# A gated block on one Trainium2 core: VectorE's calls in the block-product stage put in a new order, and two tiles of a down product added by one operation

## What is computed

```python
def _L0_ffn_ref(x, W_up, W_gate, W_down):
    wu, wg, wd = ternary_quant(W_up), ternary_quant(W_gate), ternary_quant(W_down)   # 2048x512, 2048x512, 512x2048
    up = jnp.einsum('bsd,ed->bse', x, wu)
    gate = jnp.einsum('bsd,ed->bse', x, wg)
    hidden = jax.nn.silu(up) * gate
    return jnp.einsum('bse,de->bsd', hidden, wd)
x = x + jnp.tanh(g_xattn[0]) * _L0_xattn_ref(_layernorm(x), ctx_1024, Wq, bq, Wk, bk)   # x: 4 x 512 x 512
x = x + jnp.tanh(g_ffn[0]) * _L0_ffn_ref(_layernorm(x), W_up, W_gate, W_down)
```

## Time and profile before

| | us |
|---|---|
| median of 3 runs (lowest, highest) | 394.8 (394.6, 394.83) |
| span of the profiled execution | 393.2 |
| TensorE busy | 388.2 |
| VectorE busy | 330.2 |
| ScalarE busy | 269.8 |
| GpSimd busy | 183.9 |
| granted TensorE clock, mean | 1.000 |

### The profile page before, as it was taken

The page is one execution under the profiler, slowest core; times in us unless marked ns, Lnnn a source line. Parts: engine busy times, 40 slices in busy tenths (PEclk is TensorE's granted clock), DMA queues, the critical chain, the costliest instruction groups (busy, mean ns, idle before and its releaser), DMA issues.

```text
span 393.2 us, 6214 instructions
## 1 busy us (share of the span) xinstructions
PE 388.2 (99%) x2000; PEld 219.3 (56%) x2000; DVE 330.2 (84%) x501; ACT 269.8 (69%) x366; POOL 183.9 (47%) x199
## 2 busy tenths in 40 slices
PE   8999999999999999999999999999999999999997
PEld 6676775554444444444444444556545665656886
DVE  0778897988799975789888979999999989798974
ACT  3887988899777786869897982856287566564400
POOL 0498727767845031403169462643639447261000
DMA  8999977799600030020029470006230000000014
GB/s 287 404 402 407 408 232 184 176 261 183 160 2 0 1 108 0 13 96 0 2 60 190 86 148 2 0 1 214 78 139 0 2 1 2 0 2 1 2 61 154
DMA packets 44048, 43.91 MB, mean 112 GB/s; under 512 B 30833, under 2 KB 33009, under 8 KB 42993
## 3 DMA queue, kind: packets, MB, share of 16 engines
q1 hardware_dynamic: 44016, 43.53, 36.3%
HBM read 29.89 MB, written 6.29 MB: 92 GB/s over the span
## 4 chain that ended last, share of the span: by engine, by line
PE 84%; DVE 6%; ACT 4%; issue 4%; DMA 1%; POOL 1%; DVEq 0%; ACTq 0%; POOLq 0%
PE pair L924 20%; PE pair L926 20%; PE pair L1052 14%; PE pair L1000 8%; PE pair L815 7%; PE pair L838 6%; PE pair L788 4%; PE pair L772 3%; PE pair L799 2%; DVE x_sb L1855 1%; DVE xf L1804 1%; DMA xf<-in_first 1%; PE pair L853 1%; DVE sh L1814 1%; ACT xf L1395 1%
## 5 line engine op out<-in xcount | busy, mean ns | idle before, releaser
L924 PE MATMUL pair<-xb_hi,w_sb 128*128 128x512 f16 x448 | 169.8, 379 | 0.9 <-DVE xf L1799 0.5
L926 PE MATMUL pair<-xb_lo,w_sb 128*128 128x512 f16 x448 | 169.8, 379 | 0.0
L924 PEld LDWEIGHTS pair<-xb_hi,w_sb 128*128 128x128 fp8e4 x448 | 43.8, 98 | 54.0 <-DVE xf L1799 1.3
L926 PEld LDWEIGHTS pair<-xb_lo,w_sb 128*128 128x128 fp8e4 x448 | 43.8, 98 | 49.5 <-issue 0.3
L1344 ACT ACTIVATE xf<-xf,small 128x512 f32<-128x512 f32 x48 | 34.5, 720 | 43.5 <-DVE xf L1799 23.6
L1804 DVE SCALAR_TENSOR_TENSOR xf<-xf,small 128x512 f32<-128x512 f32 x48 | 41.7, 870 | 8.5 <-ACT xf L1344 8.4
L1855 DVE SCALAR_TENSOR_TENSOR x_sb<-pair,small,x_sb 128x256 f32<-128x256 f32 (+1 forms) x85 | 37.4, 472 | 6.3 <-PE pair L1052 5.8
L1000 PE MATMUL pair<-x_sb,sh 128*128 128x512 bf16 x192 | 42.4, 379 | 0.0
L626 POOL TENSOR_TENSOR w_sb<-w_sb 128x512 fp8e4<-128x512 fp8e4 x8 | 8.8, 1101 | 55.1 <-ACT w_sb L1215 55.1
L1000 PEld LDWEIGHTS pair<-x_sb,sh 128*128 128x128 f16 x192 | 18.8, 98 | 22.6 <-DVE x_sb L1839 0.2
L1809 DVE TENSOR_TENSOR sh<-xf,sh 128x512 f16<-128x512 f32 x34 | 30.6, 906 | 0.9 <-ACT sh L1357 0.8
(11 more groups left out here) (207 smaller groups left out, 769.2 us busy)
## 6 DMA issues: line engine op xcount, KB each, us to landing
w_sb<-in_wugT SPq DMA_DIRECT2D x8, 1024.0 KB, 14.9
x_sb<-in_x SPq DMA_DIRECT2D x4, 1024.0 KB, 12.8
xf<-in_wdT SPq DMA_DIRECT2D x4, 1024.0 KB, 7.5
xt_sb<-in_wdT SPq DMA_DIRECT2D x4, 1024.0 KB, 4.9
xt_sb<-in_xT SPq DMA_DIRECT2D x12, 256.0 KB, 5.8
x_dram<-x_sb SPq DMA_DIRECT2D x8, 256.0 KB, 3.5
out<-x_sb SPq DMA_DIRECT2D x8, 256.0 KB, 4.2
x_sb<-x_dram SPq DMA_DIRECT2D x4, 512.0 KB, 3.9
```

The lines of the kernel that those rows point to most:

```text
L924: pe.matmul(dst[:, m * 512:(m + 1) * 512], w[:, o:o + P], hi[:, k], start=start and k == 0, stop=False, skip_group_check=not start)
L926: last = pe.matmul(dst[:, m * 512:(m + 1) * 512], w[:, o:o + P], lo[:, k], start=False, stop=k == 1, skip_group_check=not start)
```

## The change

The loops of every engine's part are written out as straight lists of calls. On TensorE, ScalarE, GpSimd and SyncE the instructions and their order are the same as before, with some waits stated once more or once less. On VectorE they are not:

- in units 0 to 15 the order of `norm_x1`, `ternary_down`, `low_h`, `low_s`, `low_t`, the sums of down weights and the evictions is new; `ternary_down` is split in `ternary_below` and `ternary_above`, and `weights_1` in `weights_t1` and `weights_t3`, so that other calls stand between;
- the 28 single evictions of group 2 become 14 operations `final_evict_two`, each for two tiles.

```diff
-            def ternary_down(e):
+            def ternary_below(e):
...
+                dve.tensor_scalar(t_tmp, xt_flat[:, e * DM:(e + 1) * DM], nthr[:, 2:3], None, ALU.is_lt).then_inc(s_beld, 1)
+
+            def ternary_above(e):
+
                 hold(dve, s_beld, e + 1)
...
+            def final_evict_two(j, t):
+
+                dve.wait_ge(s_fin, fin_done(2, j, t + 1))
+                if j == 5:
+                    hold(dve, s_shift, NT + t + 2)
+                elif j in (2, 3, 7):
+                    hold(dve, s_ef, fin_done(2, {2: 1, 3: 6, 7: 5}[j], t + 1))
+                b, c = TARGET[j]
+                o = (b * NT + t) * DM
+                both = x_sb[:, o:o + 2 * DM].rearrange("p (i n) -> p i n", i=2)[:, :, c * 256:(c + 1) * 256]
+                o = 0 if j in (1, 6, 7, 4) else 512
+                at = ps_c[t // 2][:, o:o + 512].rearrange("p (i n) -> p i n", i=2)
+                dve.scalar_tensor_tensor(both, at, c_out[:, :], both, ALU.mult, ALU.add).then_inc(s_ef, 2)
...
-            def evict_two(n, j):
-                for t in (2 * (n - G0 - 1), 2 * (n - G0 - 1) + 1):
-                    final_evict(2, j, t)
...
+            final_evict_two(1, 0)
+            final_evict_two(5, 0)
```

More of the change, by code:

```diff
@@ L766, in _ @@
+            low_s(14, "S4")
         @block.tensor
@@ L1098, in _ @@
[L1098 to L1133, removed]
+                    pe.wait_ge(s_ef, fin_done(g, {6: 1, 7: 6, 4: 7, 3: 5, 2: 3}[j], t | 1 if g == 2 else t))
@@ new lines, in _ @@
+            add_12(0)
+            low_h(0, "11")
+            make_h(0, "12")
+            add_22(0)
+            ternary_below(0)
+            norm_x1(3, 0)
+            make_h(0, "22")
+            add_11(1)
+            low_h(0, "12")
+            low_h(0, "22")
+            make_h(0, "21")
+            ternary_above(0)
+            make_h(1, "11")
+            add_12(1)
+            low_h(0, "21")
+            add_22(1)
+            low_h(1, "11")
+            make_h(1, "12")
+            make_h(1, "22")
@@ new lines, in _ @@
+            ternary_above(3)
+            make_h(3, "11")
+            add_12(3)
+            evict_half(3, 0)
+            low_h(3, "11")
+            make_h(3, "12")
+            evict_half(3, 1)
+            low_h(2, "22")
+            evict_half(3, 2)
+            evict_half(3, 3)
+            add_22(3)
+            make_h(3, "22")
+            norm_x1(3, 1)
+            low_h(2, "21")
+            add_11(4)
+            low_h(3, "12")
+            make_h(3, "21")
+            make_h(4, "11")
@@ new lines, in _ @@
+            norm_x1(3, 2)
+            add_12(4)
+            low_h(3, "21")
+            evict_half(4, 0)
+            low_h(3, "22")
+            make_h(4, "12")
+            evict_half(4, 1)
+            low_h(4, "11")
+            evict_half(4, 2)
+            evict_half(4, 3)
+            low_h(4, "12")
+            add_22(4)
+            make_h(4, "22")
+            add_11(5)
+            low_h(4, "22")
+            norm_x1(3, 3)
+            block_t3()
+            make_h(4, "21")
+            make_h(5, "11")
@@ new lines, in _ @@
+            make_h(7, "12")
+            block_low("T2")
+            evict_half(7, 2)
+            evict_half(7, 3)
+            low_h(7, "11")
+            add_22(7)
+            low_h(6, "21")
+            low_s(6, "S1")
+            block_low("B22")
+            low_h(6, "22")
+            make_h(7, "22")
+            weights_t1(2)
+            add_11(8)
+            weights_t3(2)
+            weights_t2(2)
+            low_s(6, "S2")
+            block_low("T4")
+            make_h(7, "21")
@@ new lines, in _ @@
+            final_evict(0, 2, 0)
+            make_h(12, "22")
+            final_evict(0, 4, 0)
+            make_h(12, "21")
+            low_h(12, "11")
+            weights_t1(1)
+            final_evict(0, 1, 1)
+            add_11(13)
+            low_s(12, "S1")
+            final_evict(0, 5, 1)
+            make_h(13, "11")
+            add_12(13)
+            final_evict(0, 6, 1)
+            low_h(12, "21")
+            final_evict(0, 3, 1)
+            make_h(13, "12")
+            add_22(13)
```

1290 lines of the change are left out of this document (800 added, 490 removed).

## The result

The changed kernel takes 395.7 us, median of 10 runs (395.3 to 396.91), beside 394.7 (393.87 to 394.89) for the kernel before on the same chip: a ratio of 1.0033, 95% interval 1.0022 to 1.0044. It is 1.0 us slower. The profiled execution of the changed kernel took 395.52 us, its span is 393.7.

A forecast was written before the change was run, and what follows sets the result against it. TensorE, busy 388.2 of 393.2 us, was taken as the bound. The terms -2.07 + 1.75 + 0.45 + 0.15 gave +0.28 us, so 394.8 became 395.1 us, with a range of 393.8 to 396.2.

The forecast's parts named there:

- within 0.2%: The outcome that a measurement cannot tell from no change, 394.0 to 395.6 us; given a chance of 0.50.
- rival 1: GpSimd's sum L626 issues before ternary_below(0): loss near 111 us 2.7 in place of 1.75, 396.0 us; chance 0.28.
- The six gaps: TensorE's waits behind 230.11, 247.69, 257.81, 260.90, 281.95 and 297.56 us, all taken as gone: -2.07 us.
- The merge: Two evictions as one on VectorE, 250 to 285 us: 0.11 us saved each of 14 times, 1.6 of VectorE.
- Place 1: Two operations put into VectorE's idle time behind 105.93 us make add_11(1) late; TensorE stands 1.75 us at 111 us.
- and starts at 106.77: VectorE reaches ternary_below(0) at about 106.2, its DMA lands at 106.7, and the compare starts at 106.77 us.
- My own case: Compare ahead of L626 by some 0.05 us, TensorE standing 1.75 at 111 us, total 395.1 us; chance 0.48.
- Place 3: low_h(10, "21") now ahead of add_22(11), near 292 us, makes TensorE wait: new loss taken as 0.45 us.
- The rest of the order: Where norm_x1(3, 1) to (3, 3), low_t, weights_t1 to weights_t4 and the low parts stand: cost 0.15 us.
- Rival 3: The six gaps stay, 240 to 300 us: +2.2 us at most, 397.0, half of it 395.9; chance 0.07.
- Rival 2: DMA lands 0.4 or more earlier, or operations slip past each other: TensorE loses 0.13 to 0.5, 393.8 us; chance 0.17.

The follow-up runs named there:

- e9: e1 with the 28 single evictions in place of the 14 merged ones; 392.94 us, ratio 0.9958 to the kernel before.
- e8: The kernel before with the new VectorE order only around add_22(0), compare and norm_x1(3, 0) behind it; 397.72 us, ratio 1.0076 to the kernel before.
- e4: The changed kernel, but GpSimd's sums of unit 2 wait until add_11(1) is done; 393.25 us, ratio 0.9965 to the kernel before.
- e11: The changed kernel, but GpSimd's first sum of unit 2 (L626) waits for the compare, ternary_below(0); 394.35 us, ratio 0.9989 to the kernel before.
- e1: The changed kernel with ternary_below(0) and norm_x1(3, 0) both put back behind add_11(1); 393.12 us, ratio 0.9969 to the kernel before.
- e10: The changed kernel with norm_x1(3, 0) moved ahead of ternary_below(0), the two calls swapped; 393.10 us, ratio 0.9958 to the kernel before.
- e3: The changed kernel with only norm_x1(3, 0) put back, ternary_below(0) staying; 394.31 us, ratio 1.0000 to the kernel before.

## Why the prediction was right and wrong

The forecast was +0.28 on the span and 395.1 us; measured were +1.09 in holes (−2.01 + 2.64 + 0.46) and 395.7 us. The time lies in the range, but 0.33% is more than "within 0.2%", to which I gave the most: the case that happened is rival 1, GpSimd first.

- **The six gaps, −2.07: right, −2.01**, and by the new order, the first of two reasons that I gave: e9 has it with single evictions, and they are gone. That it is the shorter piece of VectorE's queue in front of `add_22(9)` fits the gap behind 257.81; which call closed which of the others was not tried one by one. My "as well", that TensorE's lateness covers the same gaps, is false: in e8 it is late and they are all there.
- **The merge, 0.11 us a pair: the duration was right** (744 ns), and the term was off the path with the new order.
- **Place 1, +1.75: the term that was mis-sized; it measured 2.64.** The chain was right in each part: no slack at TensorE (counted from TensorE's last start ahead of the hole, `add_11(1)` ends at −1.49 before, +1.14 in the changed kernel, −1.14 in e4 and −0.49 in e11; that is 2.63, 0.35 and 1.00 later, beside holes of 2.64, 0.36 and 1.01), the idle time of 1.33 us that the DMA takes away, and what a meeting costs (rival 1's price of 2.7). The step that failed is the sentence "and starts at 106.77": I gave the time from the DMA's landing to the compare's start 0.07 us. It is 0.45 to 0.5 where VectorE sits waiting. In the changed kernel the DMA landed at 100.79 + 5.1 = 105.89 and the compare started at 106.38. With 0.07 it would have started at 105.96, ahead of L626 at 106.30; with 0.49 it comes 0.08 behind. (That it would then have been through in 0.47, with GpSimd's L620 running from 105.79, no run shows.) Two errors lay on each other here: these 0.4 us too few, and a DMA that took 5.1 us to land and not the 5.4 of before. Counted from the DMA's issue the compare started only 0.13 later than forecast, and the margin was 0.05. With the DMA as slow as before, it would have come some 0.4 behind L626. That the sum won by as little as 0.08 is chance. The trace of before had no wait of VectorE's for a DMA to read it from, and I did not mark the 0.07 as a choice. A bound from above would have put rival 1 ahead of my case.
- **Issue order decides.** Beside that rival stood what the Trainium skill, page "SBUF — State Buffer", section "Who interferes with whom", says: who issues first blocks the other. The runs agree: the same calls cost 2.64 with L626 first by 0.08, and 1.01 with it held behind the compare (e11, whose limits are told above). My own case, the compare ahead by 0.05 and two meetings behind it with a hole of 1.75, came up in no profile. That the block lasts the whole instruction is again not what rows show: in e11 L626 ends at 106.38 + 1.14 = 107.52, which is 0.95 behind the norm that it met (106.57), and it needs 1.09.
- **Place 3, +0.45: right, 0.46.**
- **The rest of the order, +0.15: nothing found.** The one hole of 0.06 at 232 us is a rest of the old gap, not a new one.
- **Rival 3, the order gives back nothing:** only a hole of 0.2 near 230 us comes and goes (0.20 in e1, 0.21 in e11, 0.07 in e9). **Rival 2, an earlier DMA:** e4 and e10 show what it would have been worth, holes of 0.36 and 0.28, inside its 0.13 to 0.5.

## What to carry to other kernels

An idle time of an engine is not free room: ask who else runs in it, on which memory, and which of the two starts first. Of two calls that go into a wait, the one that needs nothing from outside goes first and fills the wait; here swapping two lines was worth 2.6 us. When a forecast turns on a margin of 0.05 us, every handover in it needs a row or two bounds. And a stand of TensorE costs its own length at least, since what lies behind it moves along.

## What the runs showed of the hardware

- **From a DMA's landing to the compare on a waiting VectorE: 0.45 to 0.5 us.** Changed kernel 0.49 (105.89 to 106.38), e3 0.45, e4 0.45, e8 0.50, e11 0.47; it is the same instruction each time. In e10, where VectorE was busy with the norm when the DMA landed (100.26 + 5.3 = 105.56), the compare started 0.06 later. The landing is read to a tenth only; the difference of 0.4 is larger than that. The transfer's end is not what takes so long: VectorE's own record of the wait stands at the landing, and 0.4 pass behind it. Its line, of the changed kernel (L395 is `hold`; number, ns of the shortest, middle and longest, first and last start in us):

```profile
L395 DVEq EVENT_SEMAPHORE  x1: 21/21/21, 105.9 to 105.9; - x1
```

  Nor is it GpSimd: L620 ended 0.30 ahead of the compare in e4 (106.60, 106.90) and 0.04 ahead in the changed kernel (106.34, 106.38), and the time is the same. Nor is it every engine: in the kernel before, ScalarE's first instruction starts at 3.96, behind a DMA issued at 0.72 that lands 3.2 later. Why this compare starts late on an idle VectorE is open.
- **TensorE's clock after a stand.** Behind holes of 2.4 and 2.6 us the granted clock fell to 0.51 for 3.4 us in one profile (e8) and stayed at 1.00 in another (the changed kernel). Two of the ten runs of the changed kernel, 396.59 and 396.91 us, show a mean clock of 0.996 and are about 1 us longer than the rest, and so do three of e8's six. No run here shows what decides which execution is hit.
- **Meetings chain.** Once GpSimd's sums run back to back, each of these three operations of VectorE ends 0.28 to 0.55 us after the sum that it met and the next sum starts before it does: 0.48, 0.54 and 0.74 became 1.30, 1.32 and 1.58, 2.4 us for three.
